# A two-layer windowed-attention kernel: the engine loops over images are removed, and all sixteen image-layers are written out with constant waits

## What is computed

```python
xn = layer_norm(x, norm1_w, norm1_b)
win = windows_14x14(pad(xn))
q, k, v = split_heads(win @ qkv_w + qkv_b)
attn = q * scale @ k.T + rel_h[:, :, None] + rel_w[:, None, :]
out = (softmax(attn) @ v) @ proj_w + proj_b
x = x + unwindow(out)
x = x + gelu(layer_norm(x, norm2_w, norm2_b) @ fc1_w + fc1_b) @ fc2_w + fc2_b
```

## Time and profile before

| | us |
|---|---|
| median of 3 runs | 757.85 |
| lowest and highest | 756.81, 757.87 |
| span of the profiled execution, first to last instruction | 754.5 |
| outside the span, against the median | 3.35 |
| PE, DVE, ACT, POOL busy | 638.1, 480.3, 377.7, 192.6 |
| mean granted TensorE clock, share of full speed | 0.962 |

### The profile page before, as it was taken

The page is one execution under the profiler, slowest core; times in us unless marked ns, Lnnn a source line. Parts: engine busy times, 40 slices in busy tenths (PEclk is TensorE's granted clock), DMA queues, the critical chain, the costliest instruction groups (busy, mean ns, idle before and its releaser), DMA issues.

```text
span 754.5 us, 15592 instructions
## 1 busy us (share of the span) xinstructions
PE 638.1 (85%) x5152; PEld 539.4 (71%) x5152; DVE 480.3 (64%) x1211; ACT 377.7 (50%) x850; POOL 192.6 (26%) x392
## 2 busy tenths in 40 slices
PE   0868888989897898989898999989898989886765
PEld 0757776968785786968787877779696868765545
DVE  5257678576775858576777677685767776553221
ACT  1032445555564465555565555556555655554322
POOL 7003223132230313432231344031312223130100
PEclk9999699999998999999999999999999999999787
DMA  7301000000000000010000000000000000000000
GB/s 200 103 1 32 3 1 2 1 3 3 2 2 4 0 0 1 0 44 1 3 2 3 1 3 2 13 2 10 4 2 12 0 12 0 12 2 13 1 10 11
DMA packets 10382, 9.82 MB, mean 13 GB/s; under 512 B 1872, under 2 KB 9040, under 8 KB 10320
## 3 DMA queue, kind: packets, MB, share of 16 engines
q1 hardware_dynamic: 10320, 9.05, 4.2%
HBM read 7.08 MB, written 1.57 MB: 11 GB/s over the span
## 4 chain that ended last, share of the span: by engine, by line
PE 45%; issue 23%; DVE 19%; POOL 7%; ACT 2%; DMA 1%; DVEq 1%; SPq 1%; POOLq 0%; ACTq 0%
PE back L861 9%; PE front L915 7%; PE back L1083 6%; PE times_v L960 4%; PE by_query L979 3%; PE front L861 3%; PE by_key L943 3%; POOL norm_rstd L370 3%; PE stack_transposes L999 2%; PE stack_transposes L1002 2%; DVE row_max L789 2%; DVE xhat L648 2%; DVE xn_hi L656 2%; DVE xhat L646 2%; POOL pad_e L421 1%
## 5 line engine op out<-in xcount | busy, mean ns | idle before, releaser
L521 ACT ACTIVATE probs<-by_key 128x512 f32<-128x512 f32 x192 | 112.1, 593 | 139.8 <-PE by_key L943 138.0
L789 DVE TENSOR_REDUCE row_max<-by_query 128x2 f32<-128x512 f32 x192 | 131.2, 683 | 18.6 <-PE by_query L979 15.6
L979 PE MATMUL by_query<-k_stack,q_stack 128*128 128x256 f32 x384 | 87.2, 309 | 31.0 <-DVE row_max L789 19.5
L370 POOL TENSOR_TENSOR norm_rstd<-norm_var,minus_half 128x2 f32<-128x2 f32 x32 | 22.5, 703 | 288.9 <-DVE norm_var L638 288.7
L943 PE MATMUL by_key<-q_stack,k_stack 128*128 128x256 f32 x384 | 90.7, 319 | 5.4 <-DMA q_stack<-neg_top_t 4.9
L567 ACT ACTIVATE q_stack<-stack_transposes 128x256 fp32r<-128x256 f32 x160 | 61.3, 383 | 63.6 <-PE stack_transposes L1002 59.3
L979 PEld LDWEIGHTS by_query<-k_stack,q_stack 128*128 128x128 f32 x384 | 60.2, 194 | 45.4 <-DVE row_max L789 22.6
L943 PEld LDWEIGHTS by_key<-q_stack,k_stack 128*128 128x128 f32 x384 | 61.2, 195 | 28.1 <-issue 19.5
L915 PE MATMUL front<-q_t,rel_heads 96*84 96x32 f32 (+1 forms) x896 | 77.2, 249 | 1.4 <-ACT q_t L529 0.7
L915 PEld LDWEIGHTS front<-q_t,rel_heads 96*84 96x84 f32 x896 | 76.5, 162 | 2.3 <-ACT q_t L529 1.1
L999 PE MATMUL stack_transposes<-ident,q_stack_tok 128*128 128x128 f32 x384 | 75.9, 280 | 2.2 <-DVE q_stack_tok L669 2.1
(11 more groups left out here) (122 smaller groups left out, 1240.6 us busy)
## 6 DMA issues: line engine op xcount, KB each, us to landing
out<-X SPq DMA_DIRECT2D x8, 192.0 KB, 2.0
X<-in_x SPq DMA_DIRECT2D x1, 1344.0 KB, 9.7
w<-in_fc_w SPq DMA_DIRECT2D x2, 576.0 KB, 6.0
weights_in<-in_fc_w SPq DMA_DIRECT2D x2, 384.0 KB, 4.9
weights_in<-in_fc_w SPq DMA_DIRECT2D x4, 192.0 KB, 5.2
weights_in<-in_qkv_w SPq DMA_DIRECT2D x2, 288.0 KB, 3.2
weights_in<-in_qkv_w SPq DMA_DIRECT2D x4, 144.0 KB, 3.3
qkvb<-in_qkv_b SPq DMA_DIRECT2D x2, 288.0 KB, 4.5
```

What stands on the lines that cost most here:

```text
L521: act.activation(probs[h % NP][:, :, :], KB[h % 2][:, :].rearrange("p (k t) -> p k t", k=2), ACT.Exp).then_inc(s_ex, 1)
L789: dve.tensor_reduce(row_max[:, h, :], QB[:, :].rearrange("p (a t) -> p a t", a=TILES), AX, ALU.max).then_inc(s_smax, 1)
L979: last = pe.matmul(QB[:, a * TOK:(a + 1) * TOK], q_stack[par][:, h, a * P:(a + 1) * P], k_stack[par][:, h, :], start=True, stop=True)
```

## The change

The two loops go. `run` calls `static(i)` for every i from -1 to 17. No step, wait, slot, buffer or order within an iteration is touched; the eight iterations that were looped take the form of the other eleven, so that n is an integer everywhere: waits on constants, constant addresses, no empty instruction from `settle`. Four iteration bodies more stand in each engine's program (nineteen where there were fifteen).

```diff
@@ -247,15 +247,8 @@
                 items = [d for d in (-2, -1, 0, 1) if 0 <= i + d < 2 * IMAGES]
                 iteration(lambda d: (i + d, (i + d) // IMAGES, (i + d) % 2), items)
 
-            for i in range(-1, 3):
+            for i in range(-1, 2 * IMAGES + 2):
                 static(i)
-            for L in range(2):
-                first = IMAGES * L + 3
-                with eng.Fori(0, (IMAGES - 4) // 2, 1) as j:
-                    for odd in range(2):
-                        iteration(lambda d: (j * 2 + (first + odd + d), L, (first + odd + d) % 2), (-2, -1, 0, 1))
-                for i in range(first + IMAGES - 4, first + IMAGES if L == 0 else 2 * IMAGES + 2):
-                    static(i)
```

## The result

The written-out kernel takes 746.81 us (median of 4 runs, 746.6 to 747.6) against 757.86 us (4 runs, 756.81 to 759.34): a ratio of 0.9849, 95% interval 0.9825 to 0.9874. The forecast was 747.7 us in a range of 744.8 to 751.0. All ratios in this document are of fast runs; one run of the kernel before, at 1496.51 us beside `one_trip`, was slow and is left out of them.

A forecast was written before the change was run, and what follows sets the result against it. The engine-to-engine chain was taken to bound the kernel. Sequencer work (5.8 us) and layer 0's branch back (4.4 us) make 10.2 us off the 754.5 us span; with 3.35 us outside it, 747.7 us, range 744.8 to 751.0.

The forecast's parts named there:

- all intervals 40.8 to 40.9: Sign of being right: thirteen intervals from `top` to `top`, 110 to some 641 us, all 40.8 to 40.9 us.
- the 0.3 us that the forecast gave fetching as a bound: Fetching four more bodies per engine: nothing added, at most 4 x 0.08 = 0.3 us.
- the 2.5 us allowed: Written-out tail, about 103 us: shifted half-clock stretches could move it 2.5 us to either side.
- The branch back: Behind layer 0's loop branch: DVE's stall and the slowed clock after it, 4.4 us, bounds 0 to 4.4.
- the 1.08 us before `neg_top`: DVE's second pause behind layer 0's branch, after 2.50 us before `row_max`; counted in the interval of 43.97 us.
- The register work: Sequencer work in eight looped iterations: register operations and empty instructions, 0.72 us each, 5.8 us together.
- the term for the register operations of DVE: DVE, each looped iteration: 3 for `bn_stats`, 4 for `xhat`, 1 for the residual; 0.19 + 0.23 + 0.08 us.
- A: Stall comes from fetching, not the branch; straight code stalls elsewhere, only register work is gained: 752.1 us; chance 0.05.
- B: The 0.72 us an iteration isn't register work; only the branch's stall goes: 753.4 us; chance 0.03.
- C: Straight code falls behind its fetch, about 4.6 us a stop; three stops give 761.4 us; chance 0.03.
- D: Loops were unrolled anyway, so the program runs unchanged: 757.9 us; chance 0.01.

The follow-up runs named there:

- one_trip: Kernel before with each loop of two trips split into two loops of one trip, so no engine branches back; 751.94 us, ratio 0.9918.
- dve_straight: Kernel before with only DVE's program written out, the other four engines keeping their loops; 750.03 us.
- nops: Written-out kernel with the looped form's empty instructions put back on all engines in the eight formerly looped iterations; 750.81 us.
- nops_dve: Written-out kernel with the empty instructions put back on DVE alone, four an iteration, in the eight formerly looped iterations; 748.45 us.
- hat_first: Written-out kernel with PE's wait for xhat written first, ahead of the other waits before the transposes; 745.12 us, ratio 0.9823.
- hint: Kernel before with an instruction at each loop body's head telling every engine's sequencer where the branch will go; 753.72 us, ratio 0.9949.
- dve_tail: Kernel before with 128 do-nothing instructions put into DVE's program ahead of its very last operation; 760.45 us, ratio 1.0027.
- dve_looped: Kernel before with only DVE keeping its loops, the other four engines written out; 754.47 us.
- dve_head40: Kernel before with 40 do-nothing instructions put into DVE's program ahead of both loops; 756.45 us, ratio 0.9974.
- runs with 40 and 80 instructions: Kernel before with 40 or 80 do-nothing instructions in DVE's program ahead of both loops; 756.45 us and 750.81 us.
- hat_smax_first: As hat_first, and PE's wait for the row maximum stands ahead of the one for the stacks; 745.29 us, ratio 0.9816.

## Why the prediction was right

**The comparison that carried it.** The forecast said that a looped iteration would take what a written-out one takes, 40.84 us, for all eight. It came out at 40.83 to 40.96 us, 163.49 and 163.39 us for four against 163.36: 10.0 us where 10.17 was forecast. The intervals have no looped part left and nothing took its place. (The instructions are not quite the same in every stretch, as the prediction has it: iteration 2 has 326 matmuls, and one stretch of either kernel 27 operations of POOL. Their times do not show it.)

**The sum's small errors.** From the first full iteration to the tail the span lost 541.10 - 531.27 = 9.83 us. Two written-out intervals are 0.12 and 0.16 us too long (40.96 and 41.00), so that the sign "all intervals 40.8 to 40.9" was not met to the letter. The second is iteration 10, which every kernel has written out. It takes 40.83 to 40.88 us where DVE keeps its loops of two trips, and 40.94 to 41.00 where DVE's program has all nineteen bodies (after, one_trip, dve_straight, nops, nops_dve, hat_first), so it belongs to the longer program. In the trace of the kernel after, DVE's second `bn_stats` starts 0.09 us late at 153.0 us and `norm_var` 0.15 us late at 439.8 us, each with a packet of q14 0.6 to 1 us behind it. Both together are the 0.3 us that the forecast gave fetching as a bound; that they are the crossing of a block is what these places suggest, and no run shows it. The head was 0.81 us longer and the tail 0.68 shorter (102.26 against 102.94), within the 2.5 us allowed. That makes the 9.7 us of the two spans. The medians moved by 11.05 us, for a reason that the forecast had not seen: it took 3.35 us for what lies outside the span, but in the later runs of before, time and span differ by 2.0 to 2.5 us (most by 2.3) and after the change by 1.8 (746.6 against 744.8). The other 1.1 us is that the profiled execution of before, 754.5 us, was a quick one: later runs had spans of 753.9 to 758.6 us, in the middle 755 to 756. So the forecast had the span 0.5 us too short and what lies outside it 1.5 us too long; that it missed by only 0.9 us is in part that these two have opposite signs.

**The branch back: right in its sum, and now shown.** 4.4 us were forecast for the stall and the clock behind it; one_trip has 4.9, and hint, which keeps the loop, gives 4.7. The two misses of 0.5 us, here and in the register work below, cancel: they share out one measured difference. Within it a row was misread. The prediction put the 1.08 us before `neg_top` into the interval of 43.97 and gave that of 43.69 "no stall of its own". But `top`, which parts the two, starts at 236.88 us and the pause ends at 238.36, so that it lies in the second. Of that interval's 2.2 us over hint's 41.52, some 1.1 is thus a second pause of fetching, and some 1.1 is left for the clock, as an estimate. All four stalls have this pause, of 0.99 to 1.24 us (before, dve_tail, dve_looped, dve_head40). The forecast left open why layer 1 had no stall and said that the program's layout might decide it. The runs with 40 and 80 instructions show that it does.

**The register work: right in its sum, wrong in its parts.** The step "register work and empty instructions, some 0.72 us an iteration" gave the twelve operations that the profile lists for DVE 0.70 us, of which the empty ones had 0.20. The sum nearly held: 0.66 in one_trip. But the agreement was partly chance. The empty instructions of all engines are 0.49 of it; DVE's cost 0.23, about what was put down, while those of the other engines, which the forecast left without a price, cost the other 0.26, by the chain POOL's right behind the wait for `norm_var`. What was mis-sized is the term for the register operations of DVE: 0.50 forecast, and only some 0.44 - 0.23 = 0.21 measured. No run took the register operations by themselves, so that this 0.21 is a difference of runs. That most of them are covered, because the sequencer does them while the engine still works on the operation before, is argued and not shown.

**The rivals.** A (a stall of fetching that moves) and B (not register work) are refuted by one_trip. C (straight code falls behind its fetch) did not occur: in none of the six kernels that are written out as a whole does the timeline put idle time of DVE down to issue in a full iteration, though q8 went from 32 to 42 packets. What did occur in straight code was another thing, one fall of the clock behind a long wait for a transfer. D is refuted by the rows themselves: no row of the looped form is left.

## What to carry to other kernels

Where a kernel has the same body once in a loop and once written out, cut its trace by one operation of the body: the difference of the intervals is the price of the loop, whatever its parts are. Before a loop is written out, look for a pause put down to issue right behind its branch: announcing the branch or moving the body by some instructions took 4.7 and 4.8 us of the 10.0 us of the intervals here, with medians of 753.72 and 750.81 us against 746.81 without loops. On a chain of short operations, an empty instruction costs about 0.1 us wherever it stands behind a release, and a second wait some 0.06 us, so write the wait that ends last first.

## What had not been expected

- 40 instructions that do nothing, on an idle engine, moved a stall from one loop to another 330 us later: a pause of 2.5 us, one of 1 us behind it and some 1 us of clock.
- An empty instruction that takes 0.04 to 0.05 us costs about 0.1 us on the chain, and writing the wait that ends last behind the others in eight places costs 0.47 us of a 40.84 us iteration.
- TensorE's clock can fall at the start of an iteration, where PE has its pauses: one interval of hat_smax_first (43.12 instead of 40.7 us), one of dve_looped (42.46 instead of 41.3) and one of dve_head40 (43.12 instead of 41.6) have a granted clock of 0.57, 0.63 and 0.57 over 4 us there, that is a part of them at 1.2 instead of 2.4 GHz. Ten runs of dve_head40 go from 753.51 to 759.65 us, and their mean clocks go along, from 0.968 to 0.955; so much of the spread of this kernel's times goes with the clock.
